# In the shared expert's down products of the first mixture, the two bias products behind one another and one opening of the bank

## The reference, cut to what matters

```python
    def _L0_ffn_ref(hidden, router_w, router_b, sw1, sb1, sw2, sb2, rw1, rb1, rw2, rb2):
        ...
        sh = jax.nn.gelu(flat @ sw1 + sb1, approximate=False)
        shared_out = (sh @ sw2 + sb2) / N_SHARED
        h1 = jax.nn.gelu(jnp.einsum('td,edh->teh', flat, rw1) + rb1[None], approximate=False)
        expert_out = jnp.einsum('teh,ehd->ted', h1, rw2) + rb2[None]
        mixed = jnp.einsum('ted,te->td', expert_out, weights)
        return (shared_out + mixed).reshape(b, s, d)
```

## Time and profile before

| what | value |
|---|---|
| median of three runs | 1419.65 us (1418.27 to 1420.58) |
| the profiled execution | 1419.26 us |
| its span, first to last instruction | 1417.5 us |
| TensorE matmuls busy | 1343.1 us, 95% |
| VectorE busy | 938.8 us, 66% |
| ScalarE busy | 827.6 us, 58% |
| GpSimd busy | 501.8 us, 35% |
| mean granted TensorE clock | 0.985 of full speed |

### The profile page before, as it was taken

One profiled execution on the slowest core, in us unless ns is written; L12 is line 12 of the kernel. 1 busy time (PEld: TensorE's weight loads), 2 busy tenths in 40 slices (PEclk: granted clock), 3 DMA queues, 4 the chain that ended last, 5 costly groups with the idle time before them and its releaser, 6 DMA issues.

```text
span 1417.5 us, 33731 instructions
## 1 busy us (share of the span) xinstructions
PE 1343.1 (95%) x11200; PEld 1185.8 (84%) x11200; DVE 938.8 (66%) x2663; ACT 827.6 (58%) x2236; POOL 501.8 (35%) x410
## 2 busy tenths in 40 slices
PE   6687999999999999999999999999999999999767
PEld 4475888889898998989889898988989798898667
DVE  3347567576766757676675767767676776767684
ACT  4555564657556564755656476575647657564423
POOL 3306226070532607053260705326070431607100
PEclk9899999999999999999999999999999999999989
DMA  7100000000000000000000000000000000000000
GB/s 236 55 12 26 6 21 20 12 19 11 23 11 19 19 11 19 11 23 11 19 19 11 19 11 23 11 19 18 13 19 9 24 11 19 14 13 20 5 1 9
DMA packets 38528, 30.90 MB, mean 22 GB/s; under 512 B 9801, under 2 KB 37330, under 8 KB 38226
## 3 DMA queue, kind: packets, MB, share of 16 engines
q1 hardware_dynamic: 38194, 26.14, 6.3%
q10 hardware_dynamic: 288, 4.19, 0.8%
HBM read 27.94 MB, written 2.36 MB: 21 GB/s over the span
## 4 chain that ended last, share of the span: by engine, by line
PE 79%; issue 9%; DVE 3%; POOL 3%; POOLq 2%; DMA 1%; DVEq 1%; ACT 1%; SPq 0%; ACTq 0%
PE bank_F L1211 22%; PE bank_S L1094 7%; PE bank_A L1149 7%; PE bank_T L1127 7%; PE bank_T L1080 4%; PE bank_A L1140 3%; PE bank_T L1081 3%; PE bank_T L1082 3%; PE bank_F L1080 3%; PE bank_A L1080 3%; PE bank_F L1081 3%; PE bank_F L1082 3%; PE bank_A L1081 3%; PE bank_A L1082 3%; PE bank_F L1200 1%
## 5 line engine op out<-in xcount | busy, mean ns | idle before, releaser
L1211 PE MATMUL bank_F<-down,hid 128*128 128x128 f32 x2944 | 356.0, 276 | 6.8 <-DVE x L803 6.1
L1211 PEld LDWEIGHTS bank_F<-down,hid 128*128 128x128 f32 x2944 | 340.4, 192 | 16.0 <-DVE x L803 9.6
L593 ACT ACTIVATE probs<-bank_S,neg_max 128x256 f32<-128x256 f32 x512 | 235.8, 474 | 167.4 <-DVE neg_max L720 167.4
L720 DVE TENSOR_REDUCE neg_max<-bank_S 128x2 f32<-128x512 f32 x256 | 164.4, 683 | 76.5 <-PE bank_S L1094 76.5
L516 POOL TENSOR_TENSOR hid<-hid,qkv 128x1024 f32<-128x1024 f32 x60 | 169.0, 2829 | 11.3 <-ACT hid L609 11.3
L803 DVE SCALAR_TENSOR_TENSOR x<-bank_F,gates,x 128x128 f32<-128x128 f32 x496 | 149.3, 342 | 34.1 <-PE bank_F L1211 25.6
L577 ACT ACTIVATE probsT<-bank_T 128x512 f32<-128x512 f32 x256 | 138.9, 601 | 55.6 <-PE bank_T L1127 55.5
L486 POOL TENSOR_TENSOR mean_sq<-sum_sq,one_over_d 128x2 f32<-128x2 f32 x16 | 3.1, 195 | 434.0 <-ACT h_row L572 434.0
L1149 PE MATMUL bank_A<-probsT,values 128*64 128x256 f32 x1024 | 140.3, 395 | 6.1 <-DVE hid L737 3.1
L504 POOL TENSOR_TENSOR hid<-qkv 128x1024 f32<-128x1024 f32 x45 | 121.0, 2688 | 59.3 <-ACT qkv L577 59.3
L1127 PE MATMUL bank_T<-ident,probs 128*128 128x128 f32 x1024 | 138.7, 279 | 0.1
(11 more groups left out here) (184 smaller groups left out, 2977.3 us busy)
## 6 DMA issues: line engine op xcount, KB each, us to landing
inv_spread<-sums_apart SPq DMA_DIRECT2D x256, 64.0 KB, 2.6
sums_apart<-sum_invT SPq DMA_DIRECT2D x512, 0.5 KB
x_row<-in_x SPq DMA_DIRECT2D x16, 128.0 KB, 2.2
hid<-in_w ACTq DMA_DIRECT2D x1, 2048.0 KB, 9.5
down<-in_w ACTq DMA_DIRECT2D x1, 2048.0 KB, 14.1
out<-x SPq DMA_DIRECT2D x16, 128.0 KB, 1.9
hid<-in_rw SPq DMA_DIRECT2D x1, 1024.0 KB, 7.4
hid<-in_wv SPq DMA_DIRECT2D x1, 512.0 KB, 3.8
```

The costliest lines, as they stand in the source:

```text
L593: ins = sc.activation(probs[:, h // 2 % 2, h % 2, t, :], unit.bank(f"S{h}")[:, t * S:(t + 1) * S], ACT.Exp, bias=neg_max[:, h, t:t + 1], a ...
L720: ve.tensor_reduce(neg_max[:, h, :], v.bank(f"S{h}")[:, :].rearrange("p (t k) -> p t k", t=NT), AX.X, ALU.max, negate=True).then_inc(max_r ...
L1211: ins = te.matmul(bank[:, (j * NT + t) * P:(j * NT + t + 1) * P], hid[:, e, k, tokens(t)], down[:, e, k, :], start=k == 0, stop=k == m - 1)
```

## The change

In `D0base` the bias product leaves the loop over the halves of tokens. First come the two halves' down products, then both bias products in a loop of their own. Only the very first product has `start`, and only the very last has `stop`. The products, their operands and their number stay, and so do the waits and the signal of the unit.

```diff
@@ -1197,8 +1197,9 @@
                     wait_drained(v, name, "WT0")
                     for t in range(NT):
                         for k in range(M0):
-                            te.matmul(bank[:, tokens(t)], hid0[:, E, k, tokens(t)], down0[:, E, k, :], start=k == 0, stop=False)
-                        ins = te.matmul(bank[:, tokens(t)], gates0T[:, tokens(t)], down0_b[:], start=False, stop=True)
+                            te.matmul(bank[:, tokens(t)], hid0[:, E, k, tokens(t)], down0[:, E, k, :], start=t == k == 0, stop=False)
+                    for t in range(NT):
+                        ins = te.matmul(bank[:, tokens(t)], gates0T[:, tokens(t)], down0_b[:], start=False, stop=t == NT - 1)
                     return ins
```

## The result

The changed kernel takes 1413.2 us, median of six runs (1412.5 to 1416.4); six runs of the kernel before, three of them those of the table above, have a median of 1421.05 us (1418.3 to 1424.0). The ratio is 0.9943, 95% interval 0.9933 to 0.9954, and a second set on another occasion gave 0.9947 (0.9932 to 0.9962). The profiled execution took 1412.94 us with a span of 1411.2, against 1417.5 before: 6.3 us less.

The account below looks back on a forecast made before the run. TensorE's summed steps were taken to bound the kernel: 15 x 0.385 = 5.8 us takes the span from 1417.5 to 1411.7, with 1.8 around it 1413.5; against the three-run median, forecast 1413.9 us, range 1412.6 to 1416.8.

Parts of the forecast that it names:

- The price of a change: Between neighbouring TensorE products of 128 and 9 rows: about 0.095 us over the change, 0.10 behind it, 0.19 in all.
- The prediction's other price: Estimate from the Trainium skill's 166 ns single-product latency against 56 ns a step: 0.16 us a change, 5 us in all.
- The unit: Eight down-product and four bias-product instructions in D0base, first start to the transposes: 2.11 us before, 1.72 after, 0.385 taken as saved.
- The unseen inner steps of the bias group: Steps between the four bias instructions now together, not in the old trace: bounds 0.11 and 0.37 us, 0.11 taken.
- rival 1: Any step between 9-row products costs 0.21 us: 0.19 saved a unit, 2.9 us in all, 1416.8 us; chance 0.07.
- Rival 3: 9-row weights cannot load during the 9-row product ahead: bias steps of 0.37 us, slower, 1424.0 us; chance 0.04.
- The flags at nothing: Opening the bank once a unit instead of once per half: neither gain nor loss, bounds -0.01 to +0.01 us.
- Rival 4: Cost hangs on a new bank half or operand pair, so reordering does nothing: 1419.7 us; chance 0.08 together with rival 2.
- What passes on: Behind the unit the full 0.385 us reaches the turn, 82.97 to 82.6 us; VectorE's idle time falls from 1.05 to 0.67.
- the first turn's wait: X2T transpose waiting for VectorE's normalisation: grows from 0.64 to about 1.0 us, so the first unit gains nothing.
- Rival 2: Gain swallowed downstream by longer TensorE waits where cover is small: 1416.8 to 1419.7, say 1418.5 us; chance 0.08 with rival 4.
- The sum: Over the whole kernel, 15 of 16 units at 0.385 us each: 5.8 us off the 1417.5 us span.

Follow-up runs that it names:

- the 128-row bias: Kernel before, same order and flags, but bias products padded with zeros from 9 to 128 rows: 1408.57 us, ratio 0.9927; once more 1407.75 us, 0.9902.
- the flags alone: Kernel before with its order kept and only the change's flags, one start at the first product and one stop at the last: ratio 0.9993.

## Why the prediction was right, point by point

- **The price of a change** (0.095 us over it and 0.10 behind, 0.19 in all). Right: the change left inside the changed unit shows the same steps, and the 128-row bias, with no change of rows, loses the surcharges. Not seen: at the exit to the transposes the price is a little lower, 0.15 us (1.02 to 0.87). The sum doesn't suffer, as that change stands before and after. The prediction's other price, an estimate of 0.16 us, is below the 0.19 measured; what the engine does in these 0.19 us no run shows.
- **The unit**, forecast 1.72 us to the transposes. Measured 1.73 by the chain and 1.72 from start to start. The unseen inner steps of the bias group, where I chose 0.11 between 0.11 and 0.37, are 0.11; rivals 1 and 3, which asked for 0.21 and 0.37, fall with the row at 442.01. Rival 3 took from the Trainium skill ("TensorE: Matmul & The Clock Gate", section "Part 3: Packing small matmuls") that a load overlaps running products only where the row group differs. This trace does not agree: the loads of the 9-row products, 0.18 us each, start 0.10 to 0.11 us apart beside them, though the products' ends are modelled.

```profile
441.69 0.18 PEld L1202 LDWEIGHTS bank_F<-down_b,x2T 9*128 9x128 f32 x1
441.79 0.30 PEld L1202 LDWEIGHTS bank_F<-down_b,x2T 9*128 9x128 f32 x2
```

- **The flags at nothing.** Right, shown by the flags alone (ratio 0.9993, the same four groups). Rival 4 falls with the 128-row bias, where bank halves and operands change as before and the surcharge is gone.
- **What passes on.** Forecast turn 82.6 us, measured 82.59; VectorE's idle time forecast 0.67, measured 0.66; the first turn's wait forecast about 1.0, measured 1.05, so that unit gave nothing, as said. Rival 2, a gain that is swallowed downstream, finds nothing to swallow in a middle turn: unit and turn are both 0.38 shorter. The kernel without bias products shows that it does begin further on, where the unit is 1.17 shorter and the turn 0.89.
- **The sum.** Forecast 5.8 us, in the span 6.3. The turns carry 0.38 each, so 5.7 for 15. Of the remaining 0.6 most lies ahead of any changed code: the first down product of the first unit stands at 109.1 instead of 109.7 in the records of its line. Over the eleven profiles of this study the unit first starts anywhere between 107.8 and 111.8, so this is scatter of the start. The medians are 7.9 us apart and the forecast ratio 0.9959 lies just outside the measured interval. Some 2 us of that are not the unit's. The prediction took its base, 1419.65 us, from three runs; from the 1421.05 of six the same sum would have given 1415.3. That the forecast time is only 0.7 us off is in part luck; the length of the turn is not. The last section shows what moves the kernel before.

## What to carry to other kernels

Where TensorE is the bound, look at the rows of neighbouring fp32 products: a product with 9 or 64 rows between full ones costs 0.19 us on each side here, together more than its own two steps of 0.11. Best make it full with zero rows in a tile that is there anyway (0.74 us a turn here); where that can't be done, put the short ones together, or beside a change that stands in any case. And before counting on a saving, read how much sooner the next engine could have begun: here, of 1.17 us taken from a unit, 0.89 passed.

## What was not expected

The runs of one kernel differ by up to 5.9 us (the kernel before, 1418.1 to 1424.0), though the steady turns of a kernel profiled twice agree to 0.03 us (82.59 and 82.56, 82.23 and 82.22), and the granted clock says something of it. Busy time by stretch, of the kernel before and then of the flags alone (same order; length; PE, PEld, DVE, ACT and POOL busy; clock; DMA):

```profile
1272.00:1340.00 68.00, 60.85 (x504) 53.10 (x505) 49.69 (x150) 31.29 (x87) 29.98 (x23) 1.00 0.05 15
```

```profile
1272.00:1340.00 68.00, 62.83 (x492) 55.21 (x491) 47.92 (x139) 31.33 (x86) 29.73 (x21) 0.92 0.05 15
```

In the second, a part of this stretch was granted the 1.2 GHz level (mean 0.92 of 2.4 GHz). In slices of ten us the two part from 1310 on, where TensorE begins to wait for other engines; before that it was busy for all of the ten us at 1.00 in both. Each fence has the kernel before first and then the flags alone:

```profile
1310.00:1320.00 10.00, 8.06 (x68) 7.62 (x67) 8.36 (x22) 3.97 (x10) 1.54 (x4) 1.00 0.01 2
1310.00:1320.00 10.00, 8.06 (x54) 7.69 (x54) 7.94 (x20) 1.68 (x4) 2.75 (x3) 0.80 0.01 3
```

The last unit then comes late:

```profile
1336.10 0.45 PE bank_F L1200 x4
1340.45 0.45 PE bank_F L1200 x4
```

From the unit ahead (1271.92 and 1273.34) to this one it is 64.18 us in the first and 67.11 in the second, 2.9 more. The spans are 1417.5 and 1421.8 us, with the steady turns equal.

This is very likely also where the medians' extra 2 us come from; for the six runs of before beside the result the clock isn't on record. I sort the runs whose mean clock is on record by it, after the fact. Where it was 0.984 or more, the medians are 1418.9 us for the kernel before (9 runs), 1413.3 for the changed one (7) and 1407.7 for the 128-row bias (4). The differences, 5.6 and 11.2 us, agree with the turns, 15 x 0.38 = 5.7 and 15 x 0.74 = 11.1. Where it was 0.981 or less, the kernel before took 1422.66 us (23 runs) and the kernel with the bias products first 1414.95 (6 of its 7 runs): 7.7 us less, against 15 x 0.54 = 8.1 by the turns. Of the kernel before, 12 of 35 runs had 0.983 or more, of the changed kernel ten of twelve, and of the eleven runs of before beside the 128-row bias's 0.9902 eight had 0.981 or less. So the changed kernel's median and that of the kernel with the bias products first stem from runs of different clock, which hides the 2 us or so between the two. Why one run gets the lower clock and another doesn't isn't shown. Of changes worth a few tenths of a per cent, the length of a turn in the profile tells more than a single time.
